# A gated two-layer transformer on one core: the second layer's values and ones in one 32-column block, its softmax sums inverted in a compact layout reached through DRAM, the first layer's biases added when PSUM is read, and a new order

## The reference

```
x = x + tanh(g_xattn[0]) * L0_xattn(ctx, ctx, layernorm(x))   # step A: q, k, v with biases; softmax over the HEADS
x = x + tanh(g_ffn[0])   * L0_ffn(layernorm(x))               # step B: silu(x Wg^T) * (x Wu^T), then Wd^T; hidden 768
x = x + tanh(g_xattn[1]) * L1_xattn(layernorm(x), ctx)        # step C: one k and one v shared by all heads; softmax over the context
x = x + tanh(g_ffn[1])   * L1_ffn(layernorm(x))               # step D: x (W + low rank)^T + b
```

## Time and profile before

| | us |
|---|---|
| median of 3 runs | 2888.66 (2888.55 to 2889.1) |
| profiled execution, its own time | 2889.29 |
| its span from the first to the last instruction | 2887.5 |
| busy: TensorE | 2813.6 |
| busy: VectorE | 2486.6 |
| busy: ScalarE | 1577.7 |
| busy: GpSimd | 1441.1 |

### The profile page before, as it was taken

One profiled execution on the slowest core, in us unless ns is written; L12 is line 12 of the kernel. 1 busy time (PEld: TensorE's weight loads), 2 busy tenths in 40 slices (PEclk: granted clock), 3 DMA queues, 4 the chain that ended last, 5 costly groups with the idle time before them and its releaser, 6 DMA issues.

```text
span 2887.5 us, 80157 instructions
## 1 busy us (share of the span) xinstructions
PE 2813.6 (97%) x33173; PEld 2461.8 (85%) x33173; DVE 2486.6 (86%) x4246; ACT 1577.7 (55%) x3031; POOL 1441.1 (50%) x1633
## 2 busy tenths in 40 slices
PE   3999999999999999999999999999999999999999
PEld 2888888888888888888888888888888888888888
DVE  5888888888888888888888888888888888888888
ACT  3555555555555555555555555555555555555555
POOL 4445545544554554454455455445545544544554
PEclk9999999999999999999999999999999999999999
DMA  2000000000000000000000000000001000000000
GB/s 72 28 20 26 27 22 28 24 29 20 25 27 20 29 24 29 20 25 27 20 28 25 24 25 25 27 20 25 27 20 29 24 29 20 25 27 20 29 24 24
DMA packets 75914, 74.99 MB, mean 26 GB/s; under 512 B 6123, under 2 KB 75009, under 8 KB 75906
## 3 DMA queue, kind: packets, MB, share of 16 engines
q1 hardware_dynamic: 75906, 74.89, 8.5%
HBM read 57.30 MB, written 17.56 MB: 26 GB/s over the span
## 4 chain that ended last, share of the span: by engine, by line
PE 70%; POOL 23%; issue 3%; ACT 3%; POOLq 1%; DVE 0%; DMA 0%; SPq 0%; DVEq 0%
PE work L845 13%; PE work L716 12%; PE work L717 10%; PE work L718 10%; POOL h_lo L309 10%; POOL zt L312 8%; PE scores L799 5%; PE work L757 4%; POOL zt L316 3%; PE work L733 3%; PE scores L810 3%; PE scores L820 2%; PE work L742 2%; ACT e L418 2%; POOL zt L319 2%
## 5 line engine op out<-in xcount | busy, mean ns | idle before, releaser
L418 ACT ACTIVATE e<-scores 120x1024 f32<-120x1024 f32 x536 | 520.1, 1023 | 261.9 <-PE scores L825 251.4
L309 POOL TENSOR_TENSOR h_lo<-h_f,h_hi 128x256 fp32r<-128x256 f32 x402 | 426.3, 1073 | 204.8 <-ACT h_hi L381 201.1
L716 PE MATMUL work<-xt_hi_B,w_hi 128*128 128x256 f32 x1608 | 474.2, 295 | 10.7 <-DVE e L548 10.7
L717 PE MATMUL work<-xt_lo_B,w_hi 128*128 128x256 f32 x1608 | 454.7, 283 | 0.0
L718 PE MATMUL work<-xt_hi_B,w_lo 128*128 128x256 f32 x1608 | 454.4, 283 | 0.0
L312 POOL TENSOR_TENSOR zt<-e 120x512 f32<-120x512 f32 x268 | 342.9, 1290 | 100.4 <-ACT e L418 100.4
L601 DVE TENSOR_TENSOR e<-e,rz 120x2048 f32<-120x2048 f32 x134 | 375.5, 2802 | 2.3
L412 ACT ACTIVATE th<-work 128x256 f32<-128x256 f32 x402 | 154.4, 384 | 393.3 <-PE work L718 393.3
L588 DVE TENSOR_REDUCE m<-scores 120x128 fp32r<-120x2048 f32 x134 | 307.0, 2291 | 63.7 <-PE scores L810 63.4
L303 POOL TENSOR_TENSOR rstd_B<-var_eps_B,minus_half 128x2 f32<-128x2 f32 x67 | 46.1, 689 | 604.1 <-DVE var_eps_B L563 604.1
L716 PEld LDWEIGHTS work<-xt_hi_B,w_hi 128*128 128x128 f32 x1608 | 306.9, 191 | 29.2 <-issue 11.4
(11 more groups left out here) (194 smaller groups left out, 7689.9 us busy)
## 6 DMA issues: line engine op xcount, KB each, us to landing
x_ln<-xp SPq DMA_DIRECT2D x67, 256.0 KB, 2.8
x_res<-xp SPq DMA_DIRECT2D x67, 256.0 KB, 2.7
y<-y_out SPq DMA_DIRECT2D x67, 256.0 KB, 2.2
ctx_f_A<-cp SPq DMA_DIRECT2D x67, 128.0 KB, 2.6
ctx_f_C<-cp SPq DMA_DIRECT2D x67, 128.0 KB, 2.1
e<-wi SPq DMA_DIRECT2D x3, 768.0 KB, 5.5
e<-wf SPq DMA_DIRECT2D x2, 512.0 KB, 3.6
w_ctx<-wc SPq DMA_DIRECT2D x1, 656.0 KB
```

Of the source, the lines that this page charges most:

```text
L309: return pool.tensor_tensor(h_lo[:, m, :], h_f[:, m % 2, :], h_hi[:, m, :].bitcast(F32), ALU.subtract)
L418: return act.activation(e[0:SC, c, 2 * h:2 * h + 2, :, :].rearrange("p a b n -> p (a b n)"), scores[0:SC, 2 * h:2 * h + 2, :].rearrange("p ...
L716: pe.matmul(out, a_hi, b_hi_, start=first, stop=False, skip_group_check=parts)
L717: pe.matmul(out, a_hi, b_lo_, start=False, stop=False, skip_group_check=parts)
```

## The change

It has four parts.

Values and ones. v1_pad (64 columns) becomes v1_one (32 columns): 16 value columns and 16 columns of ones. `attended1` gives, for each chunk, 8 products with separate halves of the bank for the two parities, so that each group of 32 partitions holds 16 rows of values and 16 of sums. ScalarE copies both banks to yz (`attended1_out`).

Sums through DRAM. SP stores one row of sums for each group of 32 partitions to a DRAM tensor, 4 rows of 1024 numbers (`store_z`), packs the values from yz into y1f with eight DMAs inside SBUF (`pack_y`), reads the sums back as 128 x 32 (`load_z`), and after VectorE's reciprocal stores them (`store_rz`) and spreads them with eight broadcasting DMAs to 128 x 512 (`spread_rz`). VectorE multiplies y1f by rz1.

Biases. Before the loop, small products bring the biases of q and k of step A onto partitions (bias_col, key_bias) and that of v into all rows (val_bias). In the loop ScalarE adds bias_col while it copies q (two instructions for one), ScalarE and VectorE add key_bias with the keys (two each for one), and VectorE, now in ScalarE's place, adds val_bias with the values. The bias products of wo0 and f1 stay.

Order. All lists are rewritten and the passes are cut at another place. Step C's product with q, and all behind it, now fall partly into the next pass; STAGES_BEHIND is 4 and the loop makes 68 passes. The loops' first waits and the initial memsets follow from it.

```diff
-INIT_POOL = 20
+INIT_POOL = 18
-STAGES_BEHIND = 3
+STAGES_BEHIND = 4
...
+        yz = sb("yz", [P, KC, 2, S])
+        y1f = sb("y1f", [P, KC, S])
+        rz1 = sb("rz1", [P, KC, S])
+        z1c = sb("z1c", [P, P // 4])
+        rz1c = sb("rz1c", [P, P // 4])
+        z_dram = nc.dram_tensor("z_rows", (RG, 2 * KC * S), F32)
+        rz_dram = nc.dram_tensor("rz_rows", (RG, 2 * KC * S), F32)
...
+            def store_z():
+                return sp.dma_start(z_dram[:, :], yz[HD:P:32, :, :, :].rearrange("r c p n -> r (c p n)"))
+
+            def load_z():
+                return sp.dma_start(z1c[:, :], z_dram[:, :].rearrange("r (k n) -> (r k) n", n=P // 4))
+
+            def store_rz():
+                return sp.dma_start(rz_dram[:, :].rearrange("r (k n) -> (r k) n", n=P // 4), rz1c[:, :])
+
+            def spread_rz():
+                for r in range(RG):
+                    of = rz_dram[r, :].rearrange("(c p n) -> p c n", c=KC, p=2)
+                    for par in range(2):
+                        at = 32 * r + HD * par
+                        sp.dma_start(rz1[at:at + HD, :, :], of[par].unsqueeze(0).to_broadcast([HD, KC, S]))\
+                            .then_inc(s["rz1_spread"], 16)
+
+            def pack_y():
+                for r in range(RG):
+                    for par in range(2):
+                        at = 32 * r + HD * par
+                        sp.dma_start(y1f[at:at + HD, :, :], yz[32 * r:32 * r + HD, :, par, :]).then_inc(s["y1_packed"], 16)
...
+                sp.wait_ge(s["yz1"], t)
+                store_z().then_inc(s["z1_stored"], 16)
+                pack_y()
+                sp.wait_ge(s["z1_stored"], 16 * t)
+                load_z().then_inc(s["z1_loaded"], 16)
                 sp.wait_ge(s["kv1_mm"], t)
                 load_ctx("C", t)
+                sp.wait_ge(s["rz1"], t)
+                store_rz().then_inc(s["rz1_stored"], 16)
+                sp.wait_ge(s["rz1_stored"], 16 * t)
+                spread_rz()
...
             def query_out(st, bank):
-                return act.activation(qt[st][:, :], bank[:, :], ACT.Copy)
+                if st == "C":
+                    return act.activation(qt[st][:, :], bank[:, :], ACT.Copy)
+                for oc in range(KC):
+                    last = act.activation(qt[st][:, oc * S:(oc + 1) * S], bank[:, oc * S:(oc + 1) * S], ACT.Identity,
+                                          bias=bias_col[:, oc:oc + 1])
+                return last
...
+            def values0_out(bank):
+                v_src, v_add = (a[0:SC, 0:D].rearrange("p (g r j) -> p g r j", r=2, j=HD) for a in (bank, val_bias))
+                dve.tensor_tensor(v0_pad[0:SC, :, 0:HD], v_src[:, :, 0, :], v_add[:, :, 0, :], ALU.add)
+                return dve.tensor_tensor(v0_pad[0:SC, :, 48:48 + HD], v_src[:, :, 1, :], v_add[:, :, 1, :], ALU.add)
...
-            def attended1(bank, v, cc):
-                return per_head(bank, lambda g, par: v[0:SC, 32 * par:32 * par + 32], cc,
-                                lambda r, par: e1[0:SC, cc, r, par, :], 0, S)
+            def attended1(bank, cc):
+
+                for par in range(2):
+                    for r in range(RG):
+                        last = pe.matmul(bank[32 * r:32 * r + 32, par * S:(par + 1) * S], v1_one[0:SC, :],
+                                         e1[0:SC, cc, r, par, :], start=True, stop=True)
+                return last
...
+                dve.wait_ge(s["rz1_spread"], 128 * t)
+                dve.wait_ge(s["y1_packed"], 128 * t)
+                dve.tensor_tensor(y1f[:, :, :], y1f[:, :, :], rz1[:, :, :], ALU.mult).then_inc(s["yC"], 1)
```

More of the change, by code:

```diff
@@ L514, in _ @@
                 .then_inc(s["b_split"], 1)
+            dve.wait_ge(s["bias_mm"], 1)
+            dve.tensor_copy(bias_col[:, :], W[3][:, 0:2 * KC]).then_inc(s["bias_col"], 1)
+            dve.tensor_copy(val_bias[:, :], W[3][:, D:2 * D])
+            dve.wait_ge(s["bias_col"], 1)
+            dve.wait_ge(s["consts"], 2)
+            for odd in range(2):
+                dve.tensor_scalar(key_bias[:, odd, :], bias_col[:, KC:2 * KC], parity[:, odd:odd + 1], None, ALU.mult)
             for r, (name, n) in enumerate(ROUNDS):
@@ L571, in keys0_odd @@
             def keys0_odd(bank):
[L572 to L573 removed]
+                for kc in range(KC):
+                    last = dve.tensor_scalar(kz0[:, 1, kc, :], bank[:, kc * P:(kc + 1) * P], parity[:, 1:2],
+                                             key_bias[:, 1, kc:kc + 1], ALU.mult, ALU.add)
+                return last
+            def values0_out(bank):
+                v_src, v_add = (a[0:SC, 0:D].rearrange("p (g r j) -> p g r j", r=2, j=HD) for a in (bank, val_bias))
+                dve.tensor_tensor(v0_pad[0:SC, :, 0:HD], v_src[:, :, 0, :], v_add[:, :, 0, :], ALU.add)
+                return dve.tensor_tensor(v0_pad[0:SC, :, 48:48 + HD], v_src[:, :, 1, :], v_add[:, :, 1, :], ALU.add)
             def keys1_odd(bank):
@@ L619, in _ @@
-                dve.wait_ge(s["G_lo"], nth(0, 6, t))
-                hidden(4, W[2]).then_inc(s["G_h"], 1)
-                dve.wait_ge(s["G_a"], nth(1, 6, t))
+                dve.wait_ge(s["res_A"], t - 1)
+                moments("B", x1, t).then_inc(s["ln_eps_B"], 1)
+                dve.wait_ge(s["yC_hi"], t)
+                low(y_lo["C"][:, :, :], y1f[:, :, :], y_hi["C"][:, :, :]).then_inc(s["yC_lo"], 1)
+                dve.wait_ge(s["M0_mm"], t)
+                key_max(0).then_inc(s["M0_max"], 1)
@@ L634, in _ @@
                 normalise(1).then_inc(s["A1_p"], 1)
+                dve.wait_ge(s["dn_mm"], nth(5, 6, t))
+                residual(x2, x1, W[2]).then_inc(s["res_B"], 1)
+                dve.wait_ge(s["res_B"], t)
+                moments("C", x2, t).then_inc(s["ln_eps_C"], 1)
+                dve.wait_ge(s["yA_hi"], t)
+                low(y_lo["A"][:, :, :], two(W[3], KC), y_hi["A"][:, :, :]).then_inc(s["yA_lo"], 1)
+                dve.wait_ge(s["z1_loaded"], 16 * t)
+                dve.reciprocal(rz1c[:, :], z1c[:, :]).then_inc(s["rz1"], 1)
@@ L696, in _ @@
             pe.wait_ge(s["ld_cst"], 16 * 10)
+            pe.wait_ge(s["b_row"], 1)
+            pe.wait_ge(s["bias_zero"], 1)
+            for i, name in enumerate(("q0", "k0")):
+                for x in range(KC):
+                    pe.matmul(W[3][:, KC * i + x:KC * i + x + 1], bias_row[:, BIAS[name] + x * P:BIAS[name] + (x + 1) * P],
+                              ident[0:1, 0:1], start=True, stop=True)
+            pe.matmul(W[3][:, D:2 * D], ones_k[0:1, 0:P].bitcast(F32), b_f[:, BIAS["v0"]:BIAS["v0"] + D],
+                      start=True, stop=True).then_inc(s["bias_mm"], 1)
             pe.matmul(W[0][0:4, 0:D], ldT_s[:, :], da_s[:, :], start=True, stop=True).then_inc(s["li_t1"], 1)
@@ L741, in values0 @@
                 for kc in range(KC):
-                    pe.matmul(bank[:, 0:D], ctx_f["A"][:, kc, :], wc_of("v0", kc * D, D), start=kc == 0, stop=False)
-                return pe.matmul(bank[:, 0:D], ones_k[:, 0:P], bias_k[:, BIAS["v0"]:BIAS["v0"] + D], start=False, stop=True)
+                    last = pe.matmul(bank[:, 0:D], ctx_f["A"][:, kc, :], wc_of("v0", kc * D, D),
+                                     start=kc == 0, stop=kc == KC - 1)
+                return last
             def keys_values1(bank):
```

477 lines of the change are left out of this document (227 added, 250 removed), and 12 rows, old and new, of the table per_pass.

## The result

The changed kernel takes **3394.75 us**, the median of 4 runs (3392.8 to 3398.92), against 2888.64 us for the kernel before in 4 runs beside it (2888.55 to 2889.1). The ratio is 1.175, 95% interval 1.1736 to 1.1771: 17.5% slower. The prediction was 3258 us in a range of 2910 to 3470, with 0.88 on slower.

The account below looks back on a forecast made before the run. TensorE's products bound the kernel before; after the change, TensorE's stretch S plus the DRAM chain L set the pass: 30.8 + 16.3 = 47.1 us, 68 x 47.1 + 55.3 = 3258 us, range 2910 to 3470.

Parts of the forecast that it names:

- With slack on every other engine: Kernel before: TensorE's products are the bound, busy 97%, VectorE 86%; work taken from TensorE comes off the pass.
- TensorE's own work, 39.33 us: TensorE's products in one pass after the change, without waits: 42.29 - 0.40 - 1.96 - 0.60 = 39.33 us.
- The break-even of 41.67 us: Pass length at which the changed kernel's 68 passes take the same time as the kernel before: 41.67 us.
- S = 30.8: TensorE's stretch from wo1 to the end of the attended blocks: 29.26 us of work plus 1.5 of waiting.
- The wait for h_lo: Last down products wait for h_lo 4 and 5, behind GpSimd's three heads_total(1) additions: 1.5 us extra, between 0 and 2.6.
- L = 16.3: Chain through DRAM from the attended blocks' end to wo1: 3.9 fixed, 6.7 issues, 5.7 landings; 10.07 us of cover.
- p: Time between starts of small DMAs that SP issues in a row: taken as 0.42 us, low 0.29, packs at 0.66 high.
- Rival 2: TensorE's clock drops after each pass's pause, costing 2.0 us: pass 49.1 us, time 3394 us; chance 0.15.
- Rival 1: SP's issues and landings hide under TensorE's 10.07 us of cover: 2830 us, or 2730 without GpSimd's wait; chance 0.10.
- 16p + 3l: Sixteen issue pitches plus three landings l of 1.9 us in the DRAM chain: 6.7 + 5.7 us; under 7.0 means faster.
- the wait before wo1: Sign in the profile after: TensorE waits for y_lo_C before the wo1 product about 4 us a pass.
- the share of 84%: Sign in the profile after: TensorE's busy share falls to near 84%; above 95% would mean the chain was hidden.

Follow-up runs that it names:

- before_biases: The kernel before, with only the q and k biases of step A added when PSUM is read, four bias products fewer a pass: 2880.54 us, ratio 0.9971.
- clock_kept_more: The changed kernel with 27 and 30 unused products added on TensorE ahead of its two long waits: 3374.43 us, ratio 1.168.
- three_edits: The changed kernel with step B's moments before VectorE's wait, six packs on ScalarE, two later on SP, sums loaded right after their store: 3168.26 us, ratio 1.095.
- packs_on_scalar: The changed kernel with the eight packing DMAs issued by ScalarE at the end of its pass instead of by SP: 3234.43 us, ratio 1.120.

## Why the prediction was right, and where not

**What bounds the kernel before.** That TensorE does, and that its stream is nearly gapless, held. "With slack on every other engine" did not hold locally. On the page VectorE has 86%, but in the stretch around the second layer's reciprocals it is nearly full, and before_biases got a quarter of its four products. The share of a whole span had hidden it. In the changed kernel the two reciprocals have left that stretch, and without the trip TensorE has no wait for VectorE in the pass shown.

**TensorE's own work, 39.33 us.** Without the trip the pass is 41.03 us, and less its two waits (0.77 and 0.60) 39.66: 0.33 more than worked out, under 1%.

**The break-even of 41.67 us.** Borne out: 41.03 us is the faster side, and that kernel is 1.55% faster.

**S = 30.8.** Measured 30.75, by other parts. The wait for h_lo was taken as 1.5 us and is 0.78; 0.24 for xn_B was not foreseen; and S without its waits is 30.75 - 0.78 - 0.24 = 29.73 for 29.26. The errors cancel, by luck.

**L = 16.3: the term that was mis-sized.** Measured 17.91. The step that failed is "I take 0.42, the nearest in number" for p. For the packs it is 0.65 us, as good as the 0.66 of the two transfers from SBUF to SBUF in the earlier trace rows; the packs are of that kind, and the row nearest in kind was the right one, not the one nearest in number. That is 8 x 0.23 = 1.8 us. The spreads come from DRAM and were 0.46, 0.3 more in all; the store 0.2 more. Against it the three landings sum to 4.97 us for 5.7, 0.7 less, the small store above all (1.42). 16.3 + 1.8 + 0.3 + 0.2 - 0.7 = 17.9.

**The sum.** 30.75 + 17.91 = 48.66 us a pass, plus 0.4 for the clock. 68 x 1.6 = 109 us of the 137 us missing are L (117 by the mean of 18.02), and 20 to 27 are the clock by clock_kept_more.

**Rival 2**, the clock at 2.0 us a pass, gave 3394 us, within 1 us of the measurement, and it was still not what happened. clock_kept_more has the clock at full and takes 3374: the clock is worth 20 us, not 136. The price was read off a restart after 10.7 us of idling and charged to every pass; in this loop the low clock after the 3.25 us pause runs out inside the next wait, and the one behind wo1 comes in 21 of 55 passes and costs about 1.0 us there. The argument against it in the prediction, that the pauses are too short, was wrong too: they do lower the clock. It was their place in the pass that made them cheap. The 1.00 that the view prints for the restart is no grant either: the first record of the clock in the trace of the kernel before is at 54.35 us, where the products' pace changes. The Trainium skill, "TensorE: Matmul & The Clock Gate", "Part 1: The HAM clock gate", has idling bring the throttled clock back: the windows above agree, with 0.50 behind a pause.

**Rival 1**, hidden transfers, needed 16p + 3l under 7.0. It is 0.63 + 5.21 + 3.23 + 4.97 = 14.0.

**What would show it.** VectorE's two waits for DMAs a pass, the wait before wo1, the share of 84% (85%): seen. The packs 0.65 apart instead of 0.4 and the load of the sums 1517.59 - 1510.88 = 6.7 us after the attended bank instead of 4.6 are the mis-sized p again. The wait before wo1 is 2.1 us, not 4, because TensorE's idle time is split: 3.25 us of it falls before the q product, behind the reciprocal's own wait, which the prediction did not name. For the length of the pass that makes no difference, since wo1 waits for the later event.

**What stays open.** Why SP's spreads get slower while ScalarE issues too (0.46 to 0.62) is not settled: it may be the issuing or the packs in flight, and no run varied only that. That three_edits has S near 31.6 us is put down to the clock by comparing its own passes, and not tested with filling products. Spreads divided over both queues, or a trip that stays in SBUF, were not tried.

## What to carry to other kernels

A round trip by DMA inside a loop is to be costed as a chain, link by link: each DMA that one queue issues adds its pitch, here as much as the landings and more, and everything behind the waiting instruction on an in-order engine is late with it. When a row of the trace has to stand in for something unseen, take the row nearest in kind (from which memory to which), not nearest in number. And an engine's share of the whole span says nothing of slack at one spot: before work is moved to it, look whether it has a gap there.

## What the runs showed of the hardware

- The issue of a DMA took SP different times for different kinds: packs from SBUF to SBUF of 32 KB were 0.65 us apart, spreads from DRAM to SBUF of the same 32 KB 0.46. What in the kind makes the difference was not varied.
- Beside ScalarE's packs, SP's spreads went from 0.46 to 0.62 us apart. ScalarE's own packs were not slowed: 0.65 us apart, as on SP alone.
- A DMA took SP longer right behind its own packs: the small second store 0.58 us in three_edits (where ScalarE issued beside it too) for 0.33 without them ahead, the load of the sums 0.49 in the kernel after for 0.34 in packs_on_scalar.
- Small transfers landed in 1.4 us (16 KB to DRAM), 1.8 us (16 and 32 KB from DRAM) and 2.0 us (32 KB from SBUF to SBUF).
- In the kernel after, TensorE's clock was at 0.50 behind the pause of 3.2 to 3.5 us in 46 of 55 middle passes, and behind wo1 in 21; after pauses of 2.0 to 2.1 us before wo1 it fell in some passes and not in others. What it cost was set by what stood behind the pause: nothing where the next event was a wait.
